# Making the second gather layer's weights inside the first gather layer instead of beside the first table

## The reference, cut to what matters

```
for l in range(n_layers):                          # 2 layers
    W = jnp.einsum('rb,bio->rio', coeffs[l], bases[l])   # 8 x 30, 30 x 256 x 256 -> 8 x 256 x 256
    h = jnp.einsum('ni,rio->rno', x, W)
    msg = h[edge_type, src] * deg_inv[dst][:, None]
    agg = jax.ops.segment_sum(msg, dst, num_segments=num_nodes)
    x_new = agg + x @ self_loops[l]
    if l < n_layers - 1:
        x_new = jax.nn.relu(x_new)
    x = x_new
```

## Time and profile before

| | |
|---|---|
| median of 3 executions | 3642.26 us (3624.54 to 3656.19) |
| profiled execution, its own time | 3671.97 us |
| its span in the profile | 3670.3 us |
| mean granted PE clock | 0.798 of full |
| PE busy | 2411.8 us (66%) |
| POOL busy | 1644.3 us (45%) |
| DVE / ACT busy | 918.3 us (25%) / 658.9 us (18%) |
| `startup` | 0 to about 381 us |
| `gnn_first` | about 382 to 2039 us |

### The profile page before, as it was taken

One profiled execution on the slowest core, in us unless ns is written; L12 is line 12 of the kernel. 1 busy time (PEld: TensorE's weight loads), 2 busy tenths in 40 slices (PEclk: granted clock), 3 DMA queues, 4 the chain that ended last, 5 costly groups with the idle time before them and its releaser, 6 DMA issues. The chain is left out here.

```text
span 3670.3 us, 37811 instructions
## 1 busy us (share of the span) xinstructions
PE 2411.8 (66%) x9589; PEld 1740.0 (47%) x9592; DVE 918.3 (25%) x2885; ACT 658.9 (18%) x1463; POOL 1644.3 (45%) x1712
## 2 busy tenths in 40 slices
PE   7999346666676666666578356666566666667288
PEld 3677234544454444444456245445445454445145
DVE  2210112222212121122123023333233233234333
ACT  4455101111111111101111101111111111110033
POOL 0000645444544444454442555555555555553444
PEclk9999678877887788788789677777777777788697
DMA  7664523333333333333332323323323323222333
GB/s 219 227 225 185 157 89 113 106 104 100 115 105 98 99 110 106 105 102 109 99 113 82 114 80 87 90 83 88 88 85 88 87 85 90 84 84 62 110 106 94
DMA packets 155520, 401.34 MB, mean 109 GB/s; under 512 B 35102, under 2 KB 86657, under 8 KB 140348
## 3 DMA queue, kind: packets, MB, share of 16 engines
q0 software_dynamic: 81648, 219.65, 20.6%
q10 hardware_dynamic: 36156, 126.22, 9.0%
q1 hardware_dynamic: 37585, 53.92, 5.4%
HBM read 262.69 MB, written 141.04 MB: 110 GB/s over the span
## 5 line engine op out<-in xcount | busy, mean ns | idle before, releaser
L486 POOL DMA_INDIRECT gnn_ring<-table,g_idx x1564 | 1508.7, 965 | 1693.2 <-PE gnn_pagg L529 925.4
L529 PE MATMUL gnn_pagg<-gnn_ring,gnn_oh 128*128 x3904 | 1120.3, 433 | 354.4 <-issue 304.4
L529 PEld LDWEIGHTS gnn_pagg<-gnn_ring,gnn_oh 128*128 128x128 f32 x3904 | 780.9, 213 | 695.0 <-issue 578.2
L513 DVE TENSOR_TENSOR gnn_oh<-gnn_col,g_dst 128x256 f32<-128x256 f32 x976 | 410.2, 426 | 1754.3 <-DVEq L48 1511.4
L714 PE MATMUL gnn_pm<-gnn_whigh,gnn_high 128*128 128x512 f32 x392 | 202.9, 518 | 496.1 <-ACT gnn_rows L768 494.4
L768 ACT COPY gnn_rows<-gnn_pm 128x512 f32<-128x512 f32 x196 | 111.1, 587 | 1330.2 <-DMA pre_bs<-in_L_gnn_bases 1086.7
L714 PEld LDWEIGHTS gnn_pm<-gnn_whigh,gnn_high 128*128 128x128 f32 x392 | 95.2, 243 | 534.3 <-ACT gnn_rows L768 513.3
L1025 ACT ACTIVATE gnn_qe<-gnn_pq,gnn_bq 128x128 f32<-128x128 f32 x98 | 36.0, 367 | 1089.7 <-remote 1042.4
L714 PE MATMUL gnn_pm<-gnn_wlow,gnn_high 128*128 128x512 f32 x392 | 189.5, 483 | 0.0
L714 PE MATMUL gnn_pm<-gnn_whigh,gnn_low 128*128 128x512 f32 x392 | 189.1, 482 | 0.0
L365 PE MATMUL pre_psum<-pre_whigh,pre_high 128*128 128x512 f32 x392 | 158.6, 404 | 10.8 <-DVE pre_low L293 6.3
(11 more groups left out here) (172 smaller groups left out, 2306.5 us busy)
## 6 DMA issues: line engine op xcount, KB each, us to landing
table<-pre_rows ACTq DMA_DIRECT2D x49, 1024.0 KB, 3.9
table<-gnn_rows ACTq DMA_DIRECT2D x48, 1024.0 KB
gnn_ring<-table,g_idx POOLq DMA_INDIRECT x1564
pre_bs<-in_L_gnn_bases SPq DMA_DIRECT2D x64, 240.0 KB
bucket<-gnn_zrow SPq DMA_DIRECT2D x16, 650.0 KB
g_xT<-bucket SPq DMA_DIRECT2D x20, 520.0 KB
x1T<-gnn_x1T ACTq DMA_DIRECT2D x49, 128.0 KB
gnn_x1T<-x1T ACTq DMA_DIRECT2D x49, 128.0 KB, 2.2
```

Source lines behind the costliest of these rows:

```text
L486: eng.indirect_dma_start(self.ring[:, q % RG, t, 0:D], None, self.g.table[self.l][:, :], bass.IndirectOffsetOnAxis(ap=self.g.idx[:, at:at ...
L513: self.nc.vector.tensor_tensor(self.oh[:, h, :, :], self.col[:, :].unsqueeze(1).to_broadcast([P, n, P]), self.g.dst[:, ds(q * TPG + h * n, ...
L529: mm = nc.tensor.matmul(pagg[:, k, 0:self.width], self.oh[:, h, i, :], self.ring[:, ds(q & (RG - 1), 1), t, 0:self.width].rearrange("p o n ...
```

## The change

`startup` makes only layer 0's weights. Layer 1's are made in `gnn_first`, in 16 pieces of 1024 columns: 8 after the sum of block 0 and 8 after the sum of block 1, on PE between `outer` and `multiply`. ACT issues the loads (four DMAs of 30 x 1024 each per piece, three pieces ahead, in halves of the second `rows` buffer and a new tile `third`), copies the two results of each piece, and writes them to `wrel` from halves of the first `rows` buffer. After the last piece ACT waits until all of `wrel` is written, issues the four DMAs that read it back into `rows`, waits for them, and rounds to `whigh`; DVE forms `wlow` behind its step of block 1; and PE waits for `wlow` before the first `multiply`, instead of before its first block. SP no longer reads W back at the stage's start, and `cf` holds one layer in either stage.

```diff
@@ startup, sync
-            for b in range(NB):
-                if b and (b % G == 0 and b // G + 2 < NCH or b % EVERY == 2 and b // EVERY < NPC):
-                    eng.wait_ge(chunk_ok, NC * b)
...
-                if b % EVERY == 2 and b // EVERY < NPC:
-                    load(NPC + b // EVERY)
@@ startup, tensor (and the same two lines in scalar, after store(b))
                 multiply(b)
-                if piece_after(b) is not None:
-                    weights(piece_after(b))
@@ gnn_first
+    PIECE = 1024
+    NPC = D * D // 4 // PIECE
+    BUF = 3
...
+        third = s.sb("third", [4 * NBASE, PIECE])
+        bs = (*(rows[0:4 * NBASE, 1, k * PIECE:(k + 1) * PIECE] for k in range(2)), third[:, :])
+        wst = [rows[0:4 * R, 0, k * PIECE:(k + 1) * PIECE] for k in range(2)]
...
+        def pieces_of(b):
+
+            return range(b * NPC // 2, (b + 1) * NPC // 2) if b < 2 else ()
@@ gnn_first, sync
-            load_weights(eng, g, rows, 1, wr_in)
+            eng.dma_start(cf[:, :], a["coeff_blocks"][:, 1, :]).then_inc(cf_in, 16)
@@ gnn_first, vector
-            for h in range(H2):
-                eng.wait_ge(split_ok, h + 1)
-                ins = V.tensor_tensor(wlow[:, h, :], rows[:, h, :], whigh[:, h, :], ALU.subtract)
-            ins.then_inc(split_ok, 1)
             eng.wait_ge(kv_in, 80)
             for b in range(NB):
                 step(b, b % 2, b > 0)
+                if b == 1:
+                    for h in range(H2):
+                        eng.wait_ge(split_ok, h + 1)
+                        ins = V.tensor_tensor(wlow[:, h, :], rows[:, h, :], whigh[:, h, :], ALU.subtract)
+                    ins.then_inc(split_ok, 1)
@@ gnn_first, tensor
+            def weights(n):
+                eng.wait_ge(bs_in[n % BUF], 64 * (n // BUF + 1))
+                for q in range(2):
+                    i = 2 * n + q
+                    if i >= 2:
+                        eng.wait_ge(w_sb, i - 1)
+                    nc.tensor.matmul(pm[0:4 * R, q, :], cf[:, :], bs[n % BUF][:, q * 512:(q + 1) * 512],
+                                     start=True, stop=True).then_inc(w_ps, 1)
...
                 project(b)
                 if prev:
                     outer(1 - k)
+                for n in pieces_of(b):
+                    weights(n)
+                if b == 1:
+                    eng.wait_ge(split_ok, H2 + 1)
                 if b < NB - 1:
                     if prev:
                         multiply(1 - k)
...
-            eng.wait_ge(split_ok, H2 + 1)
+            eng.wait_ge(cf_in, 16)
@@ gnn_first, scalar
+            def load(n):
+                for q in range(4):
+                    eng.dma_start(bs[n % BUF][q * NBASE:(q + 1) * NBASE, :],
+                                  bases_of(a, 1)[q, :, n * PIECE:(n + 1) * PIECE]).then_inc(bs_in[n % BUF], 16)
+
+            def weights(n):
+                if n >= 2:
+                    eng.wait_ge(w_out[n % 2], 16 * (n // 2))
+                for q in range(2):
+                    i = 2 * n + q
+                    eng.wait_ge(w_ps, i + 1)
+                    nc.scalar.copy(wst[n % 2][:, q * 512:(q + 1) * 512], pm[0:4 * R, q, :]).then_inc(w_sb, 1)
+                if n + BUF < NPC:
+                    load(n + BUF)
+                eng.wait_ge(w_sb, 2 * n + 2)
+                eng.dma_start(g.wrel[4 * R:8 * R, n * PIECE:(n + 1) * PIECE], wst[n % 2]).then_inc(w_out[n % 2], 16)
+
+            def split():
+
+                for k in range(2):
+                    eng.wait_ge(w_out[k], 16 * NPC // 2)
+                load_weights(eng, g, rows, 1, wr_in)
+                eng.wait_ge(wr_in, WEIGHTS_IN)
+                for h in range(H2):
+                    nc.scalar.copy(whigh[:, h, :], rows[:, h, :]).then_inc(split_ok, 1)
+                eng.wait_ge(split_ok, H2 + 1)
...
                 if prev:
                     keep(b - 1, 1 - k)
...
+                for n in pieces_of(b):
+                    weights(n)
+                if b == 1:
+                    split()
                 if prev:
                     store(b - 1, 1 - k)
...
-            eng.wait_ge(wr_in, WEIGHTS_IN)
-            for h in range(H2):
-                nc.scalar.copy(whigh[:, h, :], rows[:, h, :]).then_inc(split_ok, 1)
+            for n in range(BUF):
+                load(n)
```

More of the change, by code:

```diff
@@ L119, with bases_of @@
 WEIGHTS_IN = 16 * 4
+def bases_of(a, l):
+    return a["L0_gnn_bases"][l].rearrange("b (q i) o -> q b (i o)", q=4)
 def table_rows(g, l, b):
@@ L132, in startup @@
     NPC = D * D // 4 // PIECE
-    NW = 2 * NPC
     BUF = 3
@@ L136, in startup @@
     PARTS = (0, 4), (4, 7), (7, 8)
-    EVERY = 5
     AHEAD = 4
@@ L160, in startup @@
         idi = s.sb("idi", [P, P], I32)
-        cf = s.sb("cf", [4 * NBASE, 2, 4 * R])
+        cf = s.sb("cf", [4 * NBASE, 4 * R])
         bs = s.sb("bs", [4 * NBASE, BUF, PIECE])
@@ L183, in startup @@
         dve_own = g.dve_own
-        bases = [a["L0_gnn_bases"][l].rearrange("b (q i) o -> q b (i o)", q=4) for l in range(2)]
         block = ctx.enter_context(nc.Block())
@@ L191, in stage @@
         def stage(n):
-            if n % WB < 2 or n >= NPC:
+            if n % WB < 2:
                 return wst[:, n % 2, :]
@@ L196, in stage @@
             return xs[0:4 * R, at:at + PIECE // D, :].rearrange("p b d -> p (b d)")
-        def piece_after(b):
-            c, late = divmod(b - EVERY - 1, EVERY)
-            return NPC + c if late == 0 and 0 <= c < NPC else None
         @block.sync
@@ L212, in load @@
             def load(n):
-                l, c = divmod(n, NPC)
                 if n >= BUF:
@@ L217, in load @@
                     eng.dma_start(bs[q * NBASE:(q + 1) * NBASE, n % BUF, :],
-                                  bases[l][q, :, c * PIECE:(c + 1) * PIECE]).then_inc(bs_in[n % BUF], 16)
-            eng.dma_start(cf[:, :, :], a["coeff_blocks"]).then_inc(cf_in, 16)
+                                  bases_of(a, 0)[q, :, n * PIECE:(n + 1) * PIECE]).then_inc(bs_in[n % BUF], 16)
+            eng.dma_start(cf[:, :], a["coeff_blocks"][:, 0, :]).then_inc(cf_in, 16)
             for n in range(NPC):
@@ L230, in _ @@
             for b in range(NB):
-                if b and (b % G == 0 and b // G + 2 < NCH or b % EVERY == 2 and b // EVERY < NPC):
-                    eng.wait_ge(chunk_ok, NC * b)
                 if b % G == 0 and b // G + 2 < NCH:
+                    if b:
+                        eng.wait_ge(chunk_ok, NC * b)
                     rows_in(b // G + 2)
-                if b % EVERY == 2 and b // EVERY < NPC:
-                    load(NPC + b // EVERY)
         @block.gpsimd
@@ L351, in weights @@
                         eng.wait_ge(w_sb, i - 1)
-                    nc.tensor.matmul(psum[0:4 * R, 6 + i % 2, :], cf[:, n // NPC, :], bs[:, n % BUF, q * 512:(q + 1) * 512],
+                    nc.tensor.matmul(psum[0:4 * R, 6 + i % 2, :], cf[:, :], bs[:, n % BUF, q * 512:(q + 1) * 512],
                                      start=True, stop=True).then_inc(w_ps, 1)
@@ L395, in weights @@
             def weights(n):
-                l, c = divmod(n, NPC)
-                k, earlier = (c % 2, NPC // WB + c // 2) if l else (c % WB, c // WB)
-                if earlier:
-                    eng.wait_ge(w_out[k], 16 * earlier)
+                if n >= WB:
+                    eng.wait_ge(w_out[n % WB], 16 * (n // WB))
                 for q in range(4):
@@ L404, in weights @@
                 eng.wait_ge(w_sb, 4 * n + 4)
-                eng.dma_start(g.wrel[l * 4 * R:(l + 1) * 4 * R, c * PIECE:(c + 1) * PIECE], stage(n)).then_inc(w_out[k], 16)
+                eng.dma_start(g.wrel[0:4 * R, n * PIECE:(n + 1) * PIECE], stage(n)).then_inc(w_out[n % WB], 16)
             def high_part(b):
@@ L443, in _ @@
             for k in range(WB):
-                eng.wait_ge(w_out[k], 16 * (NPC // WB + (NPC // 2 if k < 2 else 0)))
+                eng.wait_ge(w_out[k], 16 * NPC // WB)
 class Aggregate:
@@ L577, in gnn_first @@
         own_ps, own_ok, x1T_ok = (s.sem(n) for n in ("own_ps", "own_ok", "x1T_ok"))
+        cf_in, w_ps, w_sb = (s.sem(n) for n in ("cf_in", "w_ps", "w_sb"))
+        bs_in = [s.sem(f"bs_in{k}") for k in range(BUF)]
+        w_out = [s.sem(f"w_out{k}") for k in range(2)]
         kept = [s.sem(f"kept{k}") for k in range(2)]
```

## The result

The changed kernel takes 3682.38 us (median of 4 executions, 3670.34 to 3704.85), the kernel before, on the same chip and at the same time, 3633.40 (4 executions). The ratio is 1.0133, 95% interval [1.0075, 1.0191]: slower by 1.3%. The profiled execution took 3704.85 us, its span is 3702.5 (before 3670.3).

A forecast was written before the change was run, and what follows sets the result against it. PE bounds `startup`; in the gather layer no engine is full, and POOL and PE wait on each other in a chain. -29.4 in startup and +60.5 in the layer make +31 on 3642.3: 3672 us, range 3652 to 3692 (8 in 10: 3625 to 3705).

The forecast's parts named there:

- Startup, -29.4: In `startup`: 32 matmuls in 8 pieces leave PE, all on the path, saving 29.4 us (25 to 34).
- PE's start, T' + 14: Block 0: PE starts 14 us after the changed kernel's first gather (T'), against 21.9 after it before.
- Sum and projection of block 0 by T' + 45: Start of gather layer: both done 45 us after the first gather, with 30 and 84 as ends.
- 5.6 us a matmul: Price of any full-precision matmul while POOL gathers without a break, with 0.9 and 6.0 as ends.
- 4.5 pieces hidden: Behind block 0: 9 matmuls run from T' + 45 to T' + 95, where PE and ACT would have waited.
- Quiet pieces, 4.4 each with loads: Pieces run after POOL stops: 4.4 us each with loads (3.6 to 5.0), 2.3 without, ACT's part the longer.
- Shadow 26.5 with one piece in it: From block 1's sum start until chunks 0 and 1 can be copied: 26.5 us, PE getting through about one piece.
- Behind the shadow: Block 1: seven quiet pieces 24.5 us, write, read-back, rounding and subtraction 22, then multiply, reaching T' + 195.7.
- the mark: Start of block 2's sum: moves from T + 135.2 to T' + 195.7, +60.5 us in the gather layer.
- Rival (b): Slow stretch takes block 0 as now, projection only at T' + 84: +54 us, 3696 us; chance 0.26.
- Rival (a): All moved work is hidden in the gather layer, block 2's sum stays at T' + 135: 3613 us; chance 0.08.
- slower: Whole kernel above 3679 us, chance 0.42; from 3606 to 3679 counts as the same, chance 0.55.

The follow-up runs named there:

- none: The kernel before without layer 1's eight pieces in `startup`, made nowhere; `gnn_first` reads layer 0's W instead: 3576.79 us, ratio 0.982.
- second pair: Profiles of the kernel before and the changed kernel, both unchanged, run once more: 3650.02 and 3693.60 us, ratios 0.998 and 1.012 to the kernel before.
- all0: The changed kernel with all 16 pieces behind block 0's sum and the read-back issued right behind them: 2616.66 us, 0.9982 of the kernel before.
- ring8_before: The kernel before with a ring of 8 groups in place of 16 (`RG = 8`): 2622.34 us, 1.0008 of the kernel before.
- again_before: The kernel before, unchanged, run once more: 3650.02 us, ratio 0.998.
- after: The changed kernel, unchanged, in its first profile: profiled execution 3704.85 us, median 3682.38, ratio 1.0133 to the kernel before.

## Why the prediction was right, and where its sizes were off

The sign and the mechanism held: less `startup`, a gather layer that begins later, nothing made up behind it. By steps:

- *Startup, -29.4.* Measured -26.4 in the first pair of profiles, -32.3 in the second, -30.0 in `none`. Right.
- *PE's start, T' + 14.* T' + 13.9. Right.
- *Sum and projection of block 0 by T' + 45.* This step of the sum failed: T' + 94 and 100. I had argued that a PE that starts 8 us earlier does more of the sum before things get slow. It did less: from T' + 19 on the rest of the one-hots came late, four of them 11.2 us apart, and DVE had the sum 23 us behind the last. I had kept 84 as an end, and it was beyond that.
- *5.6 us a matmul.* The price held, but for another piece of work: 11.2 us for a pair of matmuls of block 0's own sum. The two of its projection took 6.3 us, after POOL had stopped, and no piece ran in the late stretch. So "4.5 pieces hidden" became none.
- *Quiet pieces, 4.4 each with loads.* 2.8 and 2.7. The issues of four loads (1.7 us) and of the write (0.4) were counted one behind the other with the copies; the timeline shows the load issues beside them. The step mis-sized the piece by more than a third, and this made up for much of the one before: block 1's sum at T' + 121 against 112.
- *Shadow 26.5 with one piece in it.* 25, with PE's part of one piece. Right.
- *Behind the shadow.* Seven pieces and the last write 27.5, measured 22.0 with ACT's part of all eight (503.00 to 525.03); read, rounding and subtraction 19.6, measured 19.3 (to 544.32); multiply 10.7, measured 8.6 (to 552.92). The pieces again were priced too high, the rest held.

The late sum (+49 against the forecast) and the cheap pieces cancelled: block 1's sum started 9 us late, the steps behind it were 9 us shorter, and the mark came at T' + 196.1 for 195.7. That it did so within a microsecond is luck. From before to after it moved by 60.9, or 62.7 in the second pair, for 60.5.

Rival (b) had the event right, block 0's sum in the late stretch, but put the mark some 23 us too high with the same price of a piece. Rival (a), with its rule of interleaving regimes from the Trainium skill, "Perfetto Trace Analysis", section "Optimization Strategy", found no support on the 3650 chips, where every piece is exposed. On the 2620 chips the trace agrees in part: the larger ring hides 33 us of the pieces, and `all0` comes to 0.998.

At the mark the sum was +30.4 to +34.5 us, as forecast. The medians differ by 49 us in the first comparison (3682.38 - 3633.40) and by 43 in the second. So 3682.38 lies inside the range of 3652 to 3692, but above the 3679 that I had drawn as the border of "slower", which had 0.42 and not the 0.55 of "the same". The step that fell short is that I had put nothing behind the mark. In the second pair of profiles the rest of the layer is 10 us longer, the second layer 3.5, `experts` 4.4. In the first pair the rest of the layer is 26 us shorter, the second layer 25 shorter, and `experts` 49 longer, so single profiles don't settle these terms. The 45 blocks behind the mark mean 32.8 us each in the first profile of before, 32.1 in the second and 32.3 in both of the change. Whether the 10 to 15 us are the change's or the executions' stays open. I had expected the same blocks, and the scatter is as large as the term; the 33.8 us that I had named as their period was one block's and not their mean.

## What to carry to other kernels

Work moved out of a full stage is paid again where the receiving stage can't run ahead; look for what stands still while the moved work runs, here POOL behind a full ring, and count the buffer's depth in time (32 tiles more hid 33 us). A mean idle share of an engine is no cover if the idle time is a wait in a chain. Moved work and the wait that follows it belong in one place: with all pieces in one block and the read-back under the next one's gathers (and with two more buffers, on another chip) the mark came 22 us earlier than with two halves and the read-back behind both. With two buffers, on a 2620 chip, the same order was worth 10.5 us in time. And compare on more than one chip when handshakes bound a kernel: the same edit was +1.2% on one and +0.2% on another.

## What the runs showed of the hardware that I had not expected

- The same program took 2620 us on two chips and 3633 to 3710 in the other comparisons, with `startup` the same to a few us (first gather at 387 and 389 in `ring8_before` there, at 383 and 386 in the kernel before here), and the granted clock 0.93 against 0.79 to 0.81 over the span in the profiles. The difference lies from the first gather on. Why the chips differ stays open.
- On the 3650 chips block 0's sum reaches DVE 7.3 to 21.7 us after PE's closing instruction is on record while POOL gathers (7.3 in `none`, 12.6 in `again_before`, 21.7 in the first profile of before, 21.0 in `after`), and 0.2 us after it on the others. In the settled blocks ACT's first chunk copy mostly starts 2.6 to 2.9 us behind POOL's stop. The cause stays open; the records don't tell a late result from matmuls that ran later than recorded.
- ACT's DMA issues and its copies overlap: four load issues of 1.7 us in all, two copies of 0.57 us and the write's issue of 0.4 fit into 2.3 us (the piece of 464.41 to 466.69 in `after`).
- The length of `experts` goes with its granted clock: with equal work (753 or 756 matmul records) it took 243 and 246 us at 0.77, 279 at 0.64, 283 at 0.63 and 295 at 0.59. Windows over that stage (length, busy us of PE, PEld, DVE, ACT, POOL, clock, DMA), of the kernel before and of the changed kernel, in their first profiles. The 49 us between them are more than the change itself is worth, and in the second pair they are 4 (278.8 and 283.2, at 0.64 and 0.63):

```profile
3424.00:3670.00 246.00, 162.86 (x753) 98.31 (x756) 76.59 (x180) 70.80 (x240) 130.14 (x129) 0.77 0.38 114
```

```profile
3407.00:3702.00 295.00, 220.92 (x756) 133.23 (x756) 75.36 (x180) 73.79 (x240) 129.81 (x129) 0.59 0.31 95
```
